# Softmax attention and a soft-tree feed-forward on one core: TensorE's work pieces on slots of their own, the norm of the preparation one phase earlier, and the shift row turned by VectorE and sent by SyncE

## What is computed

```python
x = x + attn_a(layernorm(x))      # 16 heads of 16, with biases, no mask
x = x + ffn(layernorm(x))
x = x + attn_b(layernorm(x))      # 16 heads of 16, rotary positions, causal mask
x = x + ffn(layernorm(x))

attn: softmax(q @ k.T / 4) @ v, then @ W_o
ffn:  gate = sigmoid((x @ Wq.T) @ routers.T)            # 255 nodes
      leaf_prob = product of gate or 1 - gate down 8 levels   # 256 leaves
      (leaf_prob @ leaf_values) @ Wout.T + bias
```

## Time and profile before

| | us |
|---|---|
| median of 3 runs | 1309.14 (1306.0 to 1311.37) |
| the profiled execution, its own time | 1311.34 |
| its span, first to last instruction | 1309.6 |
| TensorE busy | 1169.9 (89%) |
| VectorE busy | 936.4 (72%) |
| ScalarE busy | 718.1 (55%) |
| GpSimd busy | 336.9 (26%) |
| mean granted TensorE clock | 0.95 |

### The profile page before, as it was taken

The page is one execution under the profiler, slowest core; times in us unless marked ns, Lnnn a source line. Parts: engine busy times, 40 slices in busy tenths (PEclk is TensorE's granted clock), DMA queues, the critical chain, the costliest instruction groups (busy, mean ns, idle before and its releaser), DMA issues.

```text
span 1309.6 us, 19252 instructions
## 1 busy us (share of the span) xinstructions
PE 1169.9 (89%) x6416; PEld 565.2 (43%) x6416; DVE 936.4 (72%) x2599; ACT 718.1 (55%) x1458; POOL 336.9 (26%) x386
## 2 busy tenths in 40 slices
PE   5799999998998989989899998989889898888986
PEld 3123344344443544345343453435444354444544
DVE  3767786857777758876787667886768867787743
ACT  3165755655465555665556555565545665464551
POOL 3011203313241121412315113240323316262220
PEclk9599999999898989999899998999989999998997
DMA  7250310312004130131302213032120402011000
GB/s 204 50 129 1 88 27 17 113 50 73 25 25 121 33 90 10 43 103 33 98 1 83 64 49 81 2 113 66 48 50 2 145 17 86 13 46 53 18 17 17
DMA packets 60977, 75.33 MB, mean 58 GB/s; under 512 B 6064, under 2 KB 46672, under 8 KB 60880
## 3 DMA queue, kind: packets, MB, share of 16 engines
q1 hardware_dynamic: 58768, 73.81, 20.2%
q0 software_dynamic: 2112, 0.30, 0.1%
HBM read 12.45 MB, written 4.19 MB: 13 GB/s over the span
## 4 chain that ended last, share of the span: by engine, by line
PE 59%; DVE 16%; ACT 6%; issue 6%; SPq 5%; DMA 4%; POOL 2%; POOLq 0%; DVEq 0%
PE ps_work L1170 16%; PE ps_out L1087 11%; PE ps_max L1031 9%; PE ps_key L1063 9%; PE ps_work L1196 8%; SPq L447 5%; PE ps_work L1141 4%; DVE ps_max L789 4%; DMA q_stack<-q_part 3%; ACT probs L700 2%; DVE neg_max L793 2%; DVE scratch L944 2%; DVE scratch L947 2%; DVE scratch L916 2%; PE ps_work L1097 2%
## 5 line engine op out<-in xcount | busy, mean ns | idle before, releaser
L700 ACT ACTIVATE probs<-ps_key 128x512 f32<-128x512 f32 (+3 forms) x1024 | 503.9, 518 | 349.7 <-PE ps_key L1063 342.4
L1031 PE MATMUL ps_max<-k_stack,q_stack 96*128 96x512 bf16 (+3 forms) x1024 | 358.0, 357 | 68.0 <-DVE neg_max L789 37.9
L793 DVE TENSOR_REDUCE neg_max<-ps_max 128x1 bf16<-128x512 f32 x512 | 328.9, 683 | 85.8 <-PE ps_max L1031 84.5
L1063 PE MATMUL ps_key<-q_stack,k_stack 97*128 97x512 bf16 (+3 forms) x1024 | 354.7, 350 | 23.2 <-ACT probs L700 14.2
L789 DVE CUSTOM_DVE_ANT_0 ps_max<-ps_max,mask_b 128x128 f32<-128x128 f32 (+3 forms) x512 | 245.6, 504 | 125.9 <-PE ps_max L1031 125.7
L1087 PE MATMUL ps_out<-probs,v_ones 128*32 128x512 f32 (+3 forms) x2048 | 244.4, 550 | 0.6 <-POOL probs L601 0.6
L1031 PEld LDWEIGHTS ps_max<-k_stack,q_stack 96*128 96x128 bf16 x1024 | 101.2, 99 | 324.5 <-DVE neg_max L789 91.7
L1063 PEld LDWEIGHTS ps_key<-q_stack,k_stack 97*128 97x128 bf16 x1024 | 101.3, 99 | 148.1 <-ACT probs L700 74.5
L601 POOL TENSOR_SCALAR_AFFINE_SELECT probs<-probs 128x512 f32<-128x512 f32 x128 | 83.7, 654 | 293.8 <-ACT probs L700 293.4
L587 POOL DMA_DIRECT2D q_stack<-shift_rows x64 | 34.7, 543 | 404.8 <-DVE shift_rows L803 320.5
L1141 PE MATMUL ps_work<-ident,scratch 128*128 128x128 f32 x384 | 63.3, 297 | 26.2 <-DMA a_v_bias<-in_a_v_bias 9.7
(11 more groups left out here) (86 smaller groups left out, 1290.4 us busy)
## 6 DMA issues: line engine op xcount, KB each, us to landing
k_stack<-k_part SPq DMA_DIRECT2D x48, 256.0 KB
q_stack<-q_part SPq DMA_DIRECT2D x48, 256.0 KB
k_stack<-k_part SPq DMA_DIRECT2D x96, 128.0 KB
q_stack<-q_part SPq DMA_DIRECT2D x96, 128.0 KB
x_in<-in_x SPq DMA_DIRECT2D x8, 512.0 KB, 4.7
x_again<-in_x SPq DMA_DIRECT2D x8, 512.0 KB, 4.6
x_moved<-x_plain SPq DMA_DIRECT2D x7, 512.0 KB, 3.3
out<-x_causal SPq DMA_DIRECT2D x7, 512.0 KB, 3.2
```

What stands on the lines that cost most here:

```text
L700: act.activation(probs[step % RING][:, j, q0:T], ps_key[slot % 2][:, 0:T - q0], ACT.Exp, scale=SCALE).then_inc(on["exp_done"], 1)
L793: dve.tensor_reduce(out=dst, in_=src, axis=AX_X, op=ALU.max, negate=True)\
L1031: pe.matmul(dst[:, 0:keys], q_stack[n % 2][0:SPLIT_ROWS, h, P * qt:P * qt + P], k_stack[n % 2][0:SPLIT_ROWS, h, 0:keys], start=True, stop= ...
L1063: pe.matmul(ps_key[slot % 2][:, 0:T - q0], k_stack[n % 2][0:STACK_ROWS, h, P * kb:P * kb + P], q_stack[n % 2][0:STACK_ROWS, h, q0:T], star ...
```

## The change

- The tables have one entry for a step with two kinds of slots: those of TensorE's pieces (a step's matmuls in two halves, transposes in one piece) and that of the other engines. `matmul_schedule` plays the first on TensorE, `schedule` the second elsewhere. A piece stands three slots or more behind the reader that makes its input, and its own reader one slot behind it.
- There is one `FINISH` table. Norm and turn for phase m stand at slots 37 to 55 of phase m-2, heads and parts from slot 1 of phase m-1, `values` at slots 26 to 46 of phase m-1. For phases 1, 3 and 15 (`ready_late`) the norm and its turn are all put at slot 0 of phase m-1.
- `turn_max` and its PSUM use are gone. `neg_max` has 32 columns, VectorE transposes it in 32x32 blocks, and SyncE issues four DMAs of 16 x 64 bytes for each shift row, in SyncE's own order. `load_x` moves from slot 0 for the next phase to slot 10 for the one after it.
- `turn_out` moves from slots 8, 24, 40, 56 to 9, 25, 41, 57.

```diff
-TURN_LAG = MIX_LAG + 4
+TURN_LAG = MIX_LAG + 5
...
+FINISH = (
+    ("bias_input", 0, (), 1), ("bias_input", 1, (), 3),
+    ("turn_attended", 0, (13,), 14), ("turn_attended", 1, (14,), 15),
+    ("project_out", 0, (18, 19), 20), ("moments", 0, (), 21),
+    ("project_out", 1, (21, 22), 23), ("moments", 1, (), 23), ("spread", 0, (), 24),
+    ("normalize", 0, (), 27), ("normalize", 1, (), 28),
+    ("turn_normed", 0, (30,), 31), ("turn_normed", 1, (31,), 32),
+    ("gates", 0, (35, 37), 38), ("gates", 1, (38, 39), 40),
+    ("leaves", 0, (), 42), ("leaves", 1, (), 43), ("leaves", 2, (), 44), ("leaves", 3, (), 45), ("leaves", 4, (), 46),
+    ("turn_leaves", 0, (49,), 50), ("turn_leaves", 1, (53,), 54),
+    ("mix", 0, (58, 59), 60), ("mix", 1, (61, 62), 63),
 )
+PREPARE = (
+    ("moments", 0, (), 37 - SLOTS), ("moments", 1, (), 38 - SLOTS), ("spread", 0, (), 39 - SLOTS),
+    ("normalize", 0, (), 47 - SLOTS), ("normalize", 1, (), 48 - SLOTS),
+    ("turn_normed", 0, (50 - SLOTS,), 51 - SLOTS), ("turn_normed", 1, (54 - SLOTS,), 55 - SLOTS),
+    ("heads_k", 0, (1, 2), 3), ("heads_k", 1, (3, 5), 6), ("heads_q", 0, (6, 7), 8), ("heads_q", 1, (10, 11), 12),
+    ("values", 0, (26, 27), 28), ("values", 1, (43, 45), 46),
 )
...
+PREPARE_CAUSAL = PREPARE + (
...
+    ("rotate_k", 0, (), 10), ("rotate_k", 1, (), 11), ("high_k", 0, (), 11), ("high_k", 1, (), 12),
...
+    ("low_k", 0, (), 16), ("low_k", 1, (), 16), ("rotate_q", 0, (), 18), ("rotate_q", 1, (), 19),
+    ("high_q", 0, (), 19), ("high_q", 1, (), 20), ("rest_q", 0, (), 20), ("rest_q", 1, (), 21),
+    ("middle_q", 0, (), 21), ("middle_q", 1, (), 22), ("low_q", 0, (), 22), ("low_q", 1, (), 23),
 )
...
+def ready_late(m):
+
+    return m in (1, AHEAD, PHASES - 1)
...
+def matmul_schedule(n):
+
+    due = {}
+    for slots, _, step, i, m in sorted(work_of(n), key=lambda w: w[1]):
+        for part, slot in enumerate(slots):
+            due.setdefault(slot, []).append((step, i, m, part))
     return due
...
+            def send_shift(n, slot):
...
+                sp.wait_ge(on["shift_row"], count.next("shift_row"))
...
+                for b in range(BLOCKS):
+                    sp.dma_start(row[:, :, b, :], shift_rows[g % 2][COLS * b:COLS * b + GROUP * TILES, :])\
+                      .then_inc(sent, DMA)
+
             def core(n, slot):
+                send_shift(n, slot)
                 if slot == 0:
...
+                    else:
+                        load_x(1)
+                if slot == 10 and n + 2 < PHASES and not causal(n + 2):
+                    load_x(n + 2)
...
-                    dve.wait_ge(on["shift_full"], count.next("shift_full"))
+                    dve.wait_ge(on["max_done"], count.of("max_done", SHIFT_LAG + 1 if n < PHASES else 0))
...
-                    dve.tensor_copy(shift_rows[h], as_rows(bank)).then_inc(on["shift_row"], 1)
+                    dve.transpose(shift_rows[h][:, :], neg_max[h][:, :]).then_inc(on["shift_row"], 1)
```

More of the change, by code:

```diff
@@ L79 @@
[L79 to L85, removed]
-)
@@ L1032, in scores @@
                           k_stack[n % 2][0:SPLIT_ROWS, h, 0:keys], start=True, stop=True).then_inc(on["scores_full"], 1)
-            def turn_max(g, begun, bank):
-                pe.wait_ge(on["max_done"], count.of("max_done", begun))
-                take(bank, "shift_row")
-                for qt in range(TILES):
-                    last = pe.transpose(as_rows(bank)[:, P * qt:P * qt + P], neg_max[g % 2][:, qt, :], ident_b[:, :])
-                last.then_inc(on["shift_full"], 1)
             def ahead(n, slot):
-                at = n, slot
                 n, unit, g, j, qt = score_unit(n, slot)
@@ L1160, in turn_leaves, with rows @@
                 turn_tiles(leaf_probs[(LEVELS - 1) % 2], i, bank)
-            def rows(turned, weight, i, bank, width, read):
-                pe.wait_ge(on["turned"], count.of("turned"))
-                take(bank, read)
-                for t in range(2):
+            def rows(turned, weight, i, bank, width, read, parts, full):
+                if 0 in parts:
+                    pe.wait_ge(on["turned"], count.of("turned"))
+                    take(bank, read)
+                for t in parts:
                     tile = slice(P * (2 * i + t), P * (2 * i + t + 1))
@@ L1185, in values, with project_out, gates @@
-            def values(m, i, n, bank):
-                rows(turned_heads, weights["b_v" if causal(m) else "a_v"], i, bank, D, "values_ready")\
-                    .then_inc(on["values_full"], 1)
+                if 1 in parts:
+                    last.then_inc(on[full], 1)
+            def project_out(m, i, n, bank, parts):
+                rows(turned_block, weights["b_o" if causal(m) else "a_o"], i, bank, D, "x_ready", parts, "added_full")
+            def gates(m, i, n, bank, parts):
+                rows(turned_block, gate_w, i, bank, NODES, "gates", parts, "gates_full")
@@ L1189, in heads, with mix, values, step @@
+            def mix(m, i, n, bank, parts):
+                rows(turned_block, leaf_w, i, bank, D, "x_ready", parts, "added_full")
+            def values(m, i, n, bank, parts):
+                rows(turned_heads, weights["b_v" if causal(m) else "a_v"], i, bank, D, "values_ready", parts, "values_full")
             def heads(which):
[L1190 removed]
+                def step(m, i, n, bank, parts):
                     weight = weights[("b_" if causal(m) else "a_") + which]
[L1193 to L1195 removed]
+                    if 0 in parts:
+                        pe.wait_ge(on["turned"], count.of("turned"))
+                        take(bank, "raw_ready")
+                    for k in parts:
@@ new lines, in heads @@
+                return step
+            steps = dict(turn_attended=turn_attended, turn_normed=turn_normed, turn_leaves=turn_leaves,
+                         project_out=project_out, gates=gates, mix=mix, values=values,
+                         heads_k=heads("k"), heads_q=heads("q"))
+            whole = range(2)
+            for step, i in PREPARE_FIRST:
+                if step in steps:
+                    steps[step](0, i, -1, bank_of[step, i, 0, -1], whole)
+            opening()
+            for n in range(PHASES):
+                due = matmul_schedule(n)
+                for slot in range(SLOTS):
+                    core(n, slot)
+                    for step, i, m, part in due.get(slot, ()):
+                        steps[step](m, i, n, bank_of[step, i, m, n], (part,))
@@ L1208, in by_pairs @@
+            closing()
+            for step, i in FINISH_LAST:
+                if step in steps:
+                    steps[step](PHASES - 1, i, PHASES, bank_of[step, i, PHASES - 1, PHASES], whole)
 def by_pairs(weight):
```

143 lines of the change are left out of this document (56 added, 87 removed).

## The result

The changed kernel takes 1296.4 us (median of 4 runs, 1290.9 to 1299.6) where the kernel before takes 1309.8 (1306.0 to 1311.4): ratio 0.991 with an interval of 0.988 to 0.994. The forecast was 1228, with a range to 1282. The direction was right; more than four fifths of the gain are missing.

A forecast was written before the change was run, and what follows sets the result against it. The prediction took TensorE to lead but be held up, it and VectorE waiting in turn. From the profiled 1311 us, 1311 - 88 - 44 + 5 + 30 + 14 gave 1228 us, range 1188 to 1282.

The forecast's parts named there:

- What bounds the kernel: Whole kernel: TensorE leads, busy for 89% of the span, but is held up; it and VectorE wait in turn.
- Part 1, -88: All 16 phases: pieces laid behind their readers cut the larger engine work summed per four slots, turn_max's gain included: -88 us.
- Part 2, -44: The 15 changes of phase: the norm a phase earlier ends TensorE's waits for the stacks and clock loss: -44 us.
- missing 7: A pair of phases: 157.0 us measured against slot sums of 149.7; the difference was taken as the wait for the stacks.
- Part 3: Shift row on SyncE: +5 us for its own path in the groups, +30 for SyncE's order at slot 32 of five phases.
- the rival that made the row late in every group: Slots 0, 16, 32, 48: row DMAs land in 5.0 us behind stack traffic, 224 us lost, time 1417; chance 6%.
- The estimate of 26 us: Shift row in all 64 groups: SyncE's first byte 0.4 us sooner than GpSimd's might give back 26 us.
- SyncE's order costs nothing: Slot 32 of plain phases: x_kept lands early and the shift row is there in time; 1193 us, chance 20%.
- VectorE takes TensorE's place: Scores' waits for maxima, leaves of causal phases: VectorE still stops TensorE, slot gain 30 instead of 88; 1285 us, chance 13%.
- Banks held by half steps: PSUM banks ps_work: half steps make TensorE wait for its own readers, time stays within 0.5%; chance 3%.
- Part 4, +14: Norms for phases 1, 3, 15 at slot 0, late x_moved and load_x(1): 7, 7 and 4 us, 4 already counted; +14, bounds 6 and 25.
- still near 200 us: Sign against the gain from re-laid pieces: TensorE's waits for VectorE's maxima, 129.6 and 97.4 us before, remaining near 200 us.

The follow-up runs named there:

- c4: c1 with SHIFT_LAG 0, load_x(1) ahead of the first row, norm spread in phase 0 alone, move at slot 33: 1195.2 us, 0.915 of the kernel before.
- c1: The changed kernel with keep at slot 28, move at 36 and stack DMAs laid behind the shift row on SyncE: 1225.9 us, 0.938 of the kernel before.
- b2: The changed kernel with the old shift row (turn_max, VectorE's copy, one DMA by GpSimd), new tables kept: 1277.7 us, 0.978 of the kernel before.
- a1: The changed kernel with SyncE issuing keep and move at slot 27, behind the shift row, instead of slot 23: 1268.0 us, 0.971 of the kernel before.
- a2: The changed kernel with GpSimd instead of SyncE issuing the shift row's four DMAs: 1299.9 us, 0.9965 of the kernel before.
- c2: c1 with SHIFT_LAG 1, load_x(1) ahead of the first row, norm spread in all three late phases: 1207.9 us, 0.925 of the kernel before.
- a5: a2 with GpSimd's four products for q laid behind its low parts for k: 1279.5 us in one run, 0.979 of the kernel before.
- b1: The kernel before with the new shift row alone (transposes, four DMAs on SyncE, no turn_max), old tables: 1336.8 us, 1.027 of the kernel before.
- a3: The changed kernel with the norm for phases 1, 3 and 15 spread over slots 0 to 8: 1293.3 us, 0.990 of the kernel before.

## Where the forecast held and where it failed

- **What bounds the kernel**: right. Of the 99.4 us between the spans of the change and of c4, TensorE's stand for the row makes 76.0 (78.0 against 2.0, matmuls alone) and its own busy time 26.8: the same 6160 matmuls take 1128.0 us at a clock of 0.931 and 1101.2 at 0.966. That is 102.8; other idle time grew by 3.4. The time was lost as stands of TensorE, and as the half clock after them.
- **Part 1, -88**: the size came true for parts 1 and 2 together, once the row doesn't disturb. The slot sums said 137.7 us for a pair of phases; c4's takes 137.2, and c1's 139.3. Phases 3 to 12 take 785.8 us before and 687.8 in c4, 98 less, where the two parts come to some 89 for them (five pairs at 12, ten changes of phase at 44/15). No run has one part without the other. What the sum did not have is that the turn's bank matters: b2 shows waits of 26.7 us for it. The transpose itself was taken at 0.15 us and takes 0.20.
- **Part 2, -44**: the mechanism is right, the price isn't shown. The stacks' wait is 9.2 us, the opening's, as forecast. But the 31 us added up the waits of weight loads and matmuls, which overlap: beyond the opening the matmuls alone stood 13.1 us, at six changes of phase and not 15. So the "missing 7" of a pair was not this wait alone, and that the sum closed was partly luck.
- **Part 3, the step that failed.** It was priced at +5 for the row's own path and +30 for SyncE's order, 35 us in all. Mending the order and content of SyncE's queue alone gave back 70 (a1 and c1), and with the earlier transpose and the opening's mend 101 (c4). The matmuls' stands for the row alone are 73 us above the kernel before, where the forecast had 30. Three terms were mis-sized.
  - The stall at slot 32 was said to be 5 us, five times: place and mechanism were right (SyncE held by x_kept, then x_moved, `low_q`, the row), but it is 8.0 to 9.7. In phase 8, counted as the prediction counts from the rotate at slot 19 (692.81), x_kept is issued at 9.1 us and not 7.2, takes 7.6 to land and not 5.7, and the row lands 5.95 after that and not 5.1: 17.5 us were added up before the landing, and "about 18" leaves 0.5 for it where the rows have 1.7 (1.92 measured). TensorE came to the slot 1.7 later than said, which took some of it back.
  - The row's own landing was taken at 1.7 us, alone: behind stack DMAs of the same queue it is 3.6 to 5.1 at slot 16 of each causal phase, which stands 3.0 to 4.4 us (17.4 in five). "+5" held that as almost nothing. The upper bound of 83 for this term, and the rival that made the row late in every group by its 5.0 us landing, were the right worry; the likeliest value was the wrong one. The row was late behind stack traffic and in the first and last phases, 22 groups of 64.
  - The clock: one us of half clock for each stall was forecast and at least 0.97 for the whole; it is about 3 us behind the stall of phase 8, and 0.931. The 26.8 us of extra busy time between the change and c4 stand against the 5 that were forecast.
- **The estimate of 26 us**, to be gained by leaving GpSimd's queue, is not borne out: the row's DMAs take a median of 1.7 us to land from SyncE and 1.5 from GpSimd (a2).
- **SyncE's order costs nothing (rival, 1193)**: refuted for the change, but its number, the forecast without part 3, is where c4 arrives, at 1195. That nearness is partly luck: c4 also has the row's earlier transpose, and its late phases cost more than part 4 said. The Trainium skill (DMA: Bandwidth & Descriptors, "Issuing engines are not separate DMA queues") says that DMAs share the 16 engines whoever starts them. The traces agree that bulk traffic delays the row from either queue: at slot 16 it landed in 3.6 to 5.1 us from SyncE and in 4.7 to 6.0 from GpSimd. But the issuing time that the Trainium skill calls usually small was 2.46 us for this row, more than its undisturbed landing.
- **VectorE takes TensorE's place (rival)**: not in the change, where its work is 11 us less and it has 17% of the chain that ended last (16% before). In c4 the matmuls wait 24.4 us for the maxima, where before they waited 44.9; but once the row is out of the way VectorE has 29% of that chain, and is the next to look at.
- **Banks held by half steps (rival)**: the change's matmuls wait only 0.9 us for `attended`. It is real where `turn_max` stays: 26.7 us in b2.
- **Part 4, +14**: right in place, low in size. TensorE stands 6.73, 8.74 and 4.63 us at slot 0 of phases 0, 2 and 14 (forecast 7, 7 and 4), and the first eight slots take 18.8, 22.4 and 17.4 us against some 10 undisturbed, 28 over: less the 4 that the slot sums hold, near the bound of 25 and not at 14. The half clock behind the stands was left out. Spreading the norm helps in phase 0 alone.
- **The signs.** Waits for VectorE's maxima "still near 200 us" were to show that part 1 is wrong. They are 218.2 us in the change (227.0 before) and even 234.7 in c4, where the gain is there. These figures are mostly those of weight loads, which may wait while matmuls run; the matmuls alone wait 44.9 before and 20.6 in the change. The sign was ill chosen.

With the forecast's 88 and 44 kept and the late phases as measured, 1311 - 88 - 44 + 25 gives 1204 without the row (the 25 is 28 less some 4). The change's 1296 is then 92 above, beside 70 to 101 from the runs. The split within that (how much belongs to the early lag, how much to the opening) is not settled, since c2 to c4 change several things at once.

## What to carry to other kernels

When a step's DMAs are moved to a queue, write that queue's program down in order, and price a small urgent DMA by its landing behind the bulk DMAs ahead of it, not by its landing alone: here 1.7 us became 3.5 to 5.8. Put waits for slow copies and bulk issues behind the urgent row; that was worth 70 us without touching a compute engine. And price a stand of TensorE with the half clock behind it: 76 us of stands went with another 27 of busy time here. Last, before waits are added up, take those of matmuls apart from those of weight loads.

## What was not expected of the hardware

- **A VectorE instruction can stand behind several GpSimd ones.** The difference of two SBUF blocks took 5.74 us, not 0.68, while GpSimd ran four products of two SBUF blocks back to back. In the change the same two meet and share (GpSimd, then VectorE):

```profile
684.75 1.28 POOL L667 TENSOR_TENSOR scratch<-scratch,cosine 128x512 f32<-128x512 f32 x1 [4.13 <-DVE scratch L984]
685.98 1.73 POOL L667 TENSOR_TENSOR scratch<-scratch,sine 128x512 f32<-128x512 f32 x1
...
685.13 1.45 DVE L995 TENSOR_TENSOR scratch<-scratch,k_part 128x512 f32<-128x512 f32 x1
```

  Here VectorE seems to run between the two products: from the first one's end at 686.0 it needs 0.6 us to 686.6, and the second product is 0.45 longer than the first. The Trainium skill (SBUF — State Buffer, "Who interferes with whom") says that the ports which the two engines share are an exclusive lock, that a VectorE instruction with two SBUF inputs contends for them with a GpSimd one that reads SBUF, and that the order of issue decides who blocks. The trace agrees that one stands while the other runs; but in a2 VectorE's instruction began at 690.59, ahead of the first product at 690.84, and got nothing until all four were done. GpSimd was then still at its fourth DMA issue (690.34 to 690.82); in the seventh case it was at another instruction. Why VectorE was passed over there and not in the change stays open.
- **The same small DMA lands late behind bulk ones, from either queue.** Last issue to landing is 1.7 us undisturbed. From SyncE it is 3.6 to 5.1 at slot 16 of the causal phases in the change and 4.1 to 5.8 at slot 32 in a1; from GpSimd (a2) 4.7 to 6.0 at slot 16 and 2.7 to 3.2 at slot 32. There GpSimd's row left 1.7 to 2.1 us behind the last of 10 stack DMAs, a1's 0.5 to 1.0 behind the last of 12, and GpSimd's DMAs go by another kind of queue (8256 packets in q0, software_dynamic, where the change has 64). So whether the queue itself matters is not settled.
- **A copy in SBUF is slowed by the DMAs ahead of it, even when they left a while ago.** x_kept's 512 KB land in 2.9 to 3.0 us with no stack DMA issued in the 16 us before, in 5.1 to 6.3 behind 16 to 18 of them (a2, a5, b1 and the kernel before) and in 7.5 to 9.1 behind 22 (the change; 6.8 to 8.9 in a3 and b2). The gap to the last one is not it: x_kept is issued 0.16 us behind it in b1 and 0.4 to 1.5 before, and lands in 5.6 to 6.3 in both.
